# Moving one transpose to the end of its step, and the load of the next x tile with it, in a two-layer graph kernel

## What is computed

```
h = max(layernorm(x), 0)
A = relu((adj + adj.T) / 2);  D = row sums of A;  L = I - D^-1/2 A D^-1/2
x = x + relu(L @ (h @ W0))                     # layer 0
h = max(layernorm(x), 0)
x = x + diag(adj) (h @ W1[0]) + triu(adj) (h @ W1[1]) + tril(adj) (h @ W1[2]) + bias
```

## Time and profile before

| | us |
|---|---|
| median of 3 runs | 1033.26 (1029.0 to 1035.67) |
| the profiled execution | 1033.5 |
| its span, first to last instruction | 1031.7 |
| TensorE busy | 950.0 (92%) |
| VectorE, ScalarE, GpSimd busy | 576.9, 497.5, 293.3 |
| TensorE's mean granted clock | 0.975 of full speed |

### The profile page before, as it was taken

How to read it: one execution, slowest core, us unless ns; L and a number is a source line. 1 busy time by engine, 2 the same in 40 slices (tenths; PEclk the granted TensorE clock), 3 DMA queues, 4 the chain that set the end, 5 groups by cost and what they waited for, 6 DMA issues and landing times.

```text
span 1031.7 us, 17707 instructions
## 1 busy us (share of the span) xinstructions
PE 950.0 (92%) x4614; PEld 795.6 (77%) x4614; DVE 576.9 (56%) x1491; ACT 497.5 (48%) x1058; POOL 293.3 (28%) x289
## 2 busy tenths in 40 slices
PE   4787879989989998999999999899999999999998
PEld 4776668777877877878787888678888888888886
DVE  5895656677666676566555666444334333433332
ACT  5986455566565565444444444424333333333331
POOL 4685233333433433344444444201001100000000
PEclk9986899999999999999999999999999999999999
DMA  8995588898888986555555555556666655555552
GB/s 236 324 334 136 194 255 267 274 314 271 291 305 266 302 291 206 165 178 167 133 168 173 171 150 161 169 186 208 186 189 190 181 179 170 159 168 168 162 166 74
DMA packets 181210, 213.73 MB, mean 207 GB/s; under 512 B 13616, under 2 KB 116016, under 8 KB 178992
## 3 DMA queue, kind: packets, MB, share of 16 engines
q1 hardware_dynamic: 171952, 196.46, 62.8%
q10 hardware_dynamic: 9216, 16.78, 4.4%
HBM read 145.04 MB, written 68.16 MB: 207 GB/s over the span
## 4 chain that ended last, share of the span: by engine, by line
PE 61%; DMA 13%; issue 8%; ACT 6%; POOL 5%; DVE 5%; SPq 2%; ACTq 0%; DVEq 0%; POOLq 0%
PE psAcc L500 16%; PE psAcc L502 16%; PE psAcc L501 16%; DMA s_dram<-C 5%; DMA xp<-g_dram 3%; POOL colacc L920 3%; DMA xp<-in_x 2%; PE psG L471 2%; DMA t_dram<-x 2%; ACT xp L630 2%; PE psG L473 2%; PE psG L472 2%; POOL n_rs L912 1%; PE psZ L433 1%; DVE hTl L851 1%
## 5 line engine op out<-in xcount | busy, mean ns | idle before, releaser
L560 ACT ACTIVATE Lh<-C 128x512 fp32r<-128x512 f32 x256 | 161.3, 631 | 294.8 <-PE psAcc L502 235.2
L500 PE MATMUL psAcc<-Xh,Lh 128*128 128x512 f32 x512 | 209.3, 409 | 6.6 <-DVE Xl L779 4.7
L502 PE MATMUL psAcc<-Xh,Ll 128*128 128x512 f32 x512 | 202.8, 396 | 0.0
L501 PE MATMUL psAcc<-Xl,Lh 128*128 128x512 f32 x512 | 202.7, 396 | 0.0
L500 PE MATMUL psAcc<-Yh,Lh 128*128 128x512 f32 x512 | 200.9, 392 | 0.0
L502 PE MATMUL psAcc<-Yh,Ll 128*128 128x512 f32 x512 | 200.2, 391 | 0.0
L501 PE MATMUL psAcc<-Yl,Lh 128*128 128x512 f32 x512 | 200.0, 391 | 0.0
L723 DVE TENSOR_TENSOR Ll<-C,Lh 128x512 fp32r<-128x512 f32 x128 | 91.0, 713 | 141.4 <-ACT Lh L560 141.3
L500 PEld LDWEIGHTS psAcc<-Xh,Lh 128*128 128x128 f32 x512 | 98.4, 192 | 25.8 <-issue 7.7
L502 PEld LDWEIGHTS psAcc<-Xh,Ll 128*128 128x128 f32 x512 | 97.9, 191 | 21.7
L501 PEld LDWEIGHTS psAcc<-Xl,Lh 128*128 128x128 f32 x512 | 98.3, 192 | 17.9
(11 more groups left out here) (124 smaller groups left out, 1489.1 us busy)
## 6 DMA issues: line engine op xcount, KB each, us to landing
C<-at_dram SPq DMA_DIRECT2D x128, 256.0 KB, 2.7
at_dram<-AT SPq DMA_DIRECT2D x16, 1088.0 KB, 6.1
R<-in_adj SPq DMA_DIRECT2D x64, 256.0 KB, 5.8
C<-in_adj SPq DMA_DIRECT2D x64, 256.0 KB, 4.2
s_dram<-C ACTq DMA_DIRECT2D x64, 256.0 KB, 4.1
g_dram<-g SPq DMA_DIRECT2D x32, 512.0 KB, 4.7
C<-s_dram SPq DMA_DIRECT2D x64, 256.0 KB, 4.3
xe<-in_x SPq DMA_DIRECT2D x32, 256.0 KB, 3.7
```

What stands on the lines that cost most here:

```text
L500: mm(acc, lh, rh[:, k, :], start=k == 0, stop=False)
L501: mm(acc, lh, rl[:, k, :], start=False, stop=False)
L502: mm(acc, ll, rh[:, k, :], start=False, stop=c < L1 and k == NB - 1).then_inc(used, 1)
L560: A(Lh[:, q, :], C[:, q, :], ACT.Relu if s.c < L1 else ACT.Copy).then_inc(lhi, 1)
```

## The change

In layer 0's steps, three things take another place. First, `turn(h2, hT)` goes from k = 7 of the next step to k = 15 of the step that makes `h2`, and the products with W1 go from k = 11 and 14 to k = 5 and 8 of the next step. Second, the tile `xp` is loaded, and its statistics taken, one step ahead: the load is now issued on ScalarE's queue right behind `yTh`, and VectorE takes the statistics as its last work of the step. Third, the orders of ScalarE, VectorE and GpSimd are rewritten round these, and the stores to `t_dram` and `g_dram` move one place forward on SyncE. The number and shapes of the matmuls stay.

```diff
--- before.py
+++ after.py
@@ SyncE
-                    if q == 2 and c < NB - 1:
-                        step_wait(sp, yT, t.of(1, 1))
-                        sp.dma_start(blocks(xp[:, :]), xv[1, bass.ds(t.of(1, 1), 1)]
-                                     .rearrange("o p b f -> (o p) b f")).then_inc(ld_xp, 16)
...
-                    if q == 3 and 2 <= c < L1 + 2:
+                    if q == 2 and 2 <= c < L1 + 2:
                         step_wait(sp, tev, t.of(4, -8 + 4))
@@ TensorE, finish(t, k)
-                if k == 7 and 2 <= c < L1 + 2:
-                    wait(pe, h2_ok, t.of(1, -1))
-                    if c <= NB:
-                        wait(pe, yThi, t.of(1, 0))
-                        wait(pe, yTlo, t.of(1, 0))
-                    wait(pe, hThi, t.of(1, -2))
-                    wait(pe, hTlo, t.of(1, -2))
-                    turn(h2, hT)
...
+                if k == 15 and 1 <= c <= L1:
+                    wait(pe, h2_ok, t.of(1, 0))
+                    if c < NB:
+                        wait(pe, yThi, t.of(1, 1))
+                        wait(pe, yTlo, t.of(1, 1))
+                    elif c >= 2:
+                        wait(pe, hThi, t.of(1, -1))
+                        wait(pe, hTlo, t.of(1, -1))
+                    turn(h2, hT)
+                if k in (5, 8) and 2 <= c < L1 + 2:
+                    if k == 5:
+                        wait(pe, hThi, t.of(1, -1))
+                        wait(pe, hTlo, t.of(1, -1))
+                    for b in ((0, 1) if k == 5 else (2, 3)):
                         f = slice(b * F, (b + 1) * F)
                         wait(pe, gev, t.of(4, -8 + b - 1))
@@ ScalarE
+                if 2 <= c < L1 + 2:
+                    wait(act, hT, t.of(1, -1))
+                    wait(act, g_ok, t.of(4, -8))
+                    A(hTh[:, :], psZ[:, :], ACT.Copy).then_inc(hThi, 1)
                 if c < NB - 1:
                     copy_T(nxt, 0)
...
+                if c < NB - 1:
+                    copy_T(nxt, 2)
+                if c < LAST - 1:
+                    split_hi(nxt, 2)
+                if c < NB:
+                    wait(act, yT, t.of(1, 1))
+                    wait(act, yw_ok, t.of(1, 0))
+                    A(yTh[:, :], psZ[:, :], ACT.Copy).then_inc(yThi, 1)
+                    if c < NB - 1:
+                        act.dma_start(blocks(xp[:, :]), xv[1, bass.ds(t.of(1, 1), 1)]
+                                      .rearrange("o p b f -> (o p) b f")).then_inc(ld_xp, 16)
@@ VectorE, before the steps
+            dve.wait_ge(ld_xp, 16)
+            stats(npn, xp, s0_st, s0_mv, s0_ve, NB + 1)
@@ VectorE, in a step
                 if 1 <= c < NB:
                     sum_T(t, NQ - 1)
-                if c < NB:
-                    wait(dve, ld_xp, t.of(16, 16))
-                    stats(npn, xp, p_st, p_mv, p_ve, t.of(1, 1))
                 if c:
                     split_lo(t, NQ - 1)
+                if 2 <= c < L1 + 2:
+                    wait(dve, hThi, t.of(1, -1))
+                    V.tensor_tensor(hTl[:, :], psZ[:, :], hTh[:, :].bitcast(F32), ALU.subtract).then_inc(hTlo, 1)
...
+                if c < NB:
+                    wait(dve, yThi, t.of(1, 1))
+                    V.tensor_tensor(yTl[:, :], psZ[:, :], yTh[:, :].bitcast(F32), ALU.subtract).then_inc(yTlo, 1)
+                if c < NB - 1:
+                    wait(dve, ld_xp, t.of(16, 32))
+                    stats(npn, xp, p_st, p_mv, p_ve, t.of(1, 1))
@@ GpSimd
                 if c < NB:
+                    if c:
+                        wait(pool, p_ve, t.of(1, 0))
+                    else:
+                        pool.wait_ge(s0_ve, NB + 1)
+                    power(npn.rs[:, :], npn.ve[:, :], mhalf[:, 0:HB]).then_inc(p_rs, 1)
                     masks(t)
-                    wait(pool, p_ve, t.of(1, 1))
-                    power(npn.rs[:, :], npn.ve[:, :], mhalf[:, 0:HB]).then_inc(p_rs, 1)
```

More of the change, by code:

```diff
@@ L463, in finish @@
                     turn(xp, yT)
-                if k in (11, 14) and 2 <= c < L1 + 2:
-                    if k == 11:
+                if k == 15 and 1 <= c <= L1:
[4 more added lines that the diff above has]
+                    elif c >= 2:
                         wait(pe, hThi, t.of(1, -1))
                         wait(pe, hTlo, t.of(1, -1))
-                    for b in ((0, 1) if k == 11 else (2, 3)):
+                    turn(h2, hT)
[4 more added lines that the diff above has]
+                    for b in ((0, 1) if k == 5 else (2, 3)):
                         f = slice(b * F, (b + 1) * F)
@@ L621, in body @@
                     A(x1[:, pe_, :], z[:, :], ACT.Relu, scale=cur_e[:, 2:3]).then_inc(r1_ok, 1)
-                if 1 <= c <= NB:
-                    wait(act, yw_ok, t.of(1, 0))
-                    A(Yh[:, bass.ds(t.of(1, -1), 1), :], psW[:, :].rearrange("p (o w) -> p o w", o=1), ACT.Copy,
-                      scale=cur_e[:, 0:1]).then_inc(prep_hi, 1)
                 if c < NB:
@@ L631, in body @@
                     last.then_inc(p_h, 1)
-                elif c < L1 + NB:
+                if 1 <= c <= NB:
+                    wait(act, yw_ok, t.of(1, 0))
+                    A(Yh[:, bass.ds(t.of(1, -1), 1), :], psW[:, :].rearrange("p (o w) -> p o w", o=1), ACT.Copy,
+                      scale=cur_e[:, 0:1]).then_inc(prep_hi, 1)
+                if NB <= c < L1 + NB:
                     prep(t)
-                if 2 <= c < L1 + 2:
-                    wait(act, hT, t.of(1, -1))
-                    wait(act, g_ok, t.of(4, -8))
-                    A(hTh[:, :], psZ[:, :], ACT.Copy).then_inc(hThi, 1)
                 if c < NB - 1:
                     copy_T(nxt, 1)
-                if c < LAST - 1:
-                    split_hi(nxt, 1)
-                if c < NB - 1:
-                    copy_T(nxt, 2)
-                if c < NB:
-                    wait(act, yT, t.of(1, 1))
-                    wait(act, yw_ok, t.of(1, 0))
-                    A(yTh[:, :], psZ[:, :], ACT.Copy).then_inc(yThi, 1)
                 if 2 <= c < L1 + 2:
@@ L651, in body @@
                 if c < LAST - 1:
-                    split_hi(nxt, 2)
+                    split_hi(nxt, 1)
                 if 1 <= c <= L1:
@@ L831, in body @@
                     V.tensor_tensor(g2l[:, :], g2[:, :], g2h[:, :].bitcast(F32), ALU.subtract).then_inc(g2l_ok, 1)
-                if c < NB - 1:
-                    sum_T(nxt, 0)
                 if c < NB:
@@ L836, in body @@
                     neg_mean(npn, p_nm)
+                if c < NB - 1:
+                    sum_T(nxt, 0)
                 if c < LAST - 1:
@@ L842, in body @@
                     V.tensor_tensor(x1[:, pe_, :], x1[:, pe_, :], xe[:, :], ALU.add).then_inc(x1_ok, 1)
+                    wait(dve, x1_ok, t.of(1, 0))
+                    stats(ne, x1[:, pe_, :], e_st, e_mv, e_ve, t.of(1, 0))
                 if 1 <= c <= NB:
@@ L848, in body @@
                                            op0=ALU.mult, op1=ALU.subtract).then_inc(prep_lo, 1)
-                if 2 <= c < L1 + 2:
-                    wait(dve, hThi, t.of(1, -1))
-                    V.tensor_tensor(hTl[:, :], psZ[:, :], hTh[:, :].bitcast(F32), ALU.subtract).then_inc(hTlo, 1)
                 if c < NB - 1:
                     sum_T(nxt, 1)
-                if 1 <= c <= L1:
-                    wait(dve, x1_ok, t.of(1, 0))
-                    stats(ne, x1[:, pe_, :], e_st, e_mv, e_ve, t.of(1, 0))
-                if c < LAST - 1:
-                    split_lo(nxt, 1)
-                if c < NB:
-                    wait(dve, yThi, t.of(1, 1))
-                    V.tensor_tensor(yTl[:, :], psZ[:, :], yTh[:, :].bitcast(F32), ALU.subtract).then_inc(yTlo, 1)
                 if 2 <= c < L1 + 2:
@@ L865, in body @@
                     t_out(t, 1)
-                if c < NB - 1:
-                    sum_T(nxt, 2)
                 if 1 <= c <= L1:
@@ L870, in body @@
                     neg_mean(ne, e_nm)
+                if c < LAST - 1:
+                    split_lo(nxt, 1)
                 if 2 <= c < L1 + 2:
@@ L874, in body @@
                     wait(dve, tev, t.of(4, -4))
+                if c < NB - 1:
+                    sum_T(nxt, 2)
                 if c < LAST - 1:
                     split_lo(nxt, 2)
+                if c < NB:
+                    wait(dve, yThi, t.of(1, 1))
+                    V.tensor_tensor(yTl[:, :], psZ[:, :], yTh[:, :].bitcast(F32), ALU.subtract).then_inc(yTlo, 1)
+                if c < NB - 1:
+                    wait(dve, ld_xp, t.of(16, 32))
+                    stats(npn, xp, p_st, p_mv, p_ve, t.of(1, 1))
                 if c >= L1:
```

2 lines of the change are left out of this document (1 added, 1 removed).

## The result

The changed kernel takes 1108.29 us (median of 4 runs, 1102.8 to 1113.29) against 1031.13 us for the kernel before on the same chip (4 runs, 1027.45 to 1035.67). The ratio is 1.0745, with a 95% interval of 1.0673 to 1.0817. The forecast was 1068, so the sign was right and the size was not: +77 us instead of +35, and past the upper end of the range. Of all the runs in this document one, of e1, was slower than its fellows at a lower granted clock (1078.57 us at 0.952): the ratios leave it out, and without it e1's median is 1059.04.

A forecast was written before the change was run, and what follows sets the result against it. TensorE, busy 92% of the span, was taken as the bound, so gains come only from its waits. First stage +47, second stage -13.5, steps 32 and 33 -5, clock +6.5: +35 on 1033.5, 1068 us; range 1040 to 1105.

The forecast's parts named there:

- The loop (c): Steps 2 to 14: `xp` landing, VectorE, second W1 pair and next load form a loop of 23.0 us against 19.6.
- The landing, 4.5 us: Time from issue to landing of the `xp` load inside the loop, taken as the tile's median, 4.5 us.
- Rival 1: The `xp` landing is short, 2.9 us; the first-stage step is 21.4 and the time 1046 us; chance 0.20.
- The clock, +6.5: TensorE runs slow behind one in three new second-pair waits, 1.4 us each: +6.5 us.
- Rival 2: TensorE's clock falls in every first-stage step behind the second pair, +3.1 instead of 0.5 a step: 1105 us; chance 0.12.
- The second stage, -13.5: Steps 17 to 31 run with hardly a wait, 0.9 us shorter each: -13.5 us over 15 steps.
- rival 3: The second stage gains nothing because `xp` from `g_dram` lands late or the earlier transposes wait elsewhere: 1082 us; chance 0.15.
- The 13.6: Predicted length in us of a second-stage step with hardly a wait, against 14.5 before.
- (a): TensorE's wait before the second W1 pair in steps 2 to 15: at least 1.8 us, where 0.6 was.
- (b): TensorE's wait for `yTl` before the transpose of `h2` at k = 15 in steps 2 to 15: 1.0 us.
- Step 15: Loads no `xp` and has no next strip, so it takes about 20.7 us, 1.1 more than before.
- steps 32 on: In steps 32 and 33 half of the waits go as the stores land earlier: -5 us.

The follow-up runs named there:

- e1: Changed kernel with VectorE's statistics of `xp` moved back behind `hTl` of the next step: 1060.79 us, ratio 1.0264 to the kernel before.
- e2: Changed kernel with the load of `xp` issued ahead of ScalarE's copy of the third quarter's transposes: 1068.82 us, ratio 1.036 to the kernel before.
- e4: Changed kernel with the stores to `t_dram` and `g_dram` back in the fourth quarter on SyncE: 1094.16 us, ratio 1.0598 to the kernel before.
- e5: Changed kernel with twelve idle matmuls added ahead of TensorE's first-pair wait in steps 2 to 15: 1109.16 us, ratio 1.0797 to the kernel before.
- e3: Changed kernel with GpSimd's power ahead of its subtraction from step 16 on: 1098.96 us, ratio 1.066 to the kernel before.
- e9: e6 with ScalarE's third-quarter copy ahead of `h2`, and `yTh`, `t_out`, `yTl` ahead of that quarter's splits: 1005.87 us, ratio 0.9724 to the kernel before.
- e6: Changed kernel with the edits of e1, e2 and e3, plus the second W1 pair at k = 13 in steps 2 to 15: 1038.19 us, ratio 1.0121.

## Why the prediction was wrong in size and right in sign

*The loop (c): right.* The place, its members and their sum to the issue held: 11.96 and 18.45 in an undisturbed step against 12.0 and 18.5. e1 and e2 show it as the cause: with the loop open, steps lose 3 to 4 us.

*The landing, 4.5 us: the first failed step.* It was 5.96 on the mean, +1.46 in each of 12 steps, 17.5 us. "I take the median landing because the company is alike" was the wrong sentence, and its second half names the reason: the stores of `t_dram` and `g_dram`, behind the load before and moved to stand just in front of it. e4 puts 1.3 us a step on them. Rival 1 went the wrong way altogether: DMA share fell from 0.84 to 0.66 and the landing became longer.

*The clock, +6.5: the second failed step, in its place and its frequency; its size came out by luck.* The 1.4 us for one slow stretch behind the second pair were right (1.3 to 1.6 in e5). But I looked for it there, one time in three; it stood behind the first pair's longer wait in 11 of 14 steps. The mean time to the issue is 19.4 against 18.45 in an undisturbed step of e5: of these 0.9 us the turn takes 0.3 and leaves about 0.6 to the slow stretches. Over 12 steps that is some 4 us and 7 us, the latter by luck near the 6.5. Rival 2 put the clock in every step and was nearest to the time, at 1105, but by another route: full price behind the second pair (+3.1 a step), which the trace does not show. Part of a stretch behind the first pair is hidden: the wait for `gev_out` behind it is 1.2 to 1.5 us, and 2.7 to 2.8 in most steps of e5, where the first pair runs at full speed.

*VectorE's loop turn: not in the sum.* 0.6 us every second step, some 4 us in all. Before, it lay in slack.

*The second stage, -13.5: the third failed step.* It became +0.7, rival 3's outcome by another cause. The load was not late and ScalarE not short; VectorE's 128x4 instruction was held by GpSimd for 0.75 us a step. I had taken GpSimd's work as covered since its results were early, and did not ask what its running does to VectorE. The 13.6 itself was sound: e3 reaches 13.81 and e9 13.73. The kernel before had such a hold elsewhere, on the pick of `cur_g` ahead of `z`, beside GpSimd's bias (one runs from 439.59 to 441.25, the pick beside it from 440.02 to 441.28). Its VectorE group in steps 17 to 31 shows it, with another instruction of the same shape:

```profile
L793 DVE COPY cur_g<-scal 128x4 f32 (+1 forms) x15 | 17.9, 1191 | 0.0
L704 DVE TENSOR_SCALAR ne_ve<-ne_mv 128x4 f32<-128x4 f32 x15 | 2.6, 170 | 0.5
```

*Waits (a) and (b).* (b) was forecast at 1.0 and is 0.8 in most steps. (a) was to be at least 1.8 in an open step and about 2.6 in the loop, and under 1.8 was to show me wrong. It is 1.2 to 1.5 in steps 5 to 14 and 0.4 in step 15, with the loop closed all the same. The sign was a bad one: TensorE comes to the second pair late behind the longer first wait (3.0 on the mean of the 14 steps, against 2.1 forecast) and the slow stretch. With the first pair's wait gone, in e1, (a) is 2.7 in most steps.

*Step 15 and steps 32 on.* Step 15 was right by TensorE's boundaries (20.66 for 20.7). Steps 32 on gave 1.4 of the 5; no run here looks into the half that I took.

By the table, the errors are 18.1 for steps 2 to 15 (30.3, less the 6.5 counted for the clock and the 5.7 of step 15, which belongs to the same loop), 14.2 for 17 to 31, 3.6 behind them and 2.0 in steps 0, 1 and 16. They add to 37.9, the distance from 1033.5 + 35.2 to the profiled execution's 1106.65.

What stays open: the clock's part in the closed loop was not removed by itself, since the filler only moved it, so its 0.6 us a step is a share worked out of mixed steps and not a difference of two times. Why the clock falls behind some waits and not behind others of the same length stays open too.

## What to carry to other kernels

When a load's issue and its consumer both come to lie on engines that the load itself holds up, the landing is a term of every step. Price it by what is issued near it, not by the tile's median, and add each small delay of the loop (a loop's turn, a clock drop) in full.

An engine that "has slack" may still hold another engine: compare the mean duration of tiny instructions of one shape between stages, and look at what runs beside the long ones.

Removing one wait uncovers the next in the chain (1108, 1061, 1038, 1006 over e1, e6 and e9); the order won only when the chain of the last remaining wait was put in front of work with slack.
